# The store of the new x moved from SyncE to ScalarE in the finishes of the first three layers

## The chip, the cores and the metric

The kernel runs on one core of one Trainium2 chip. The metric is the device time of one execution in microseconds, the median of several runs. Engines: TensorE (PE in the profile, its weight loads PEld), VectorE (DVE), ScalarE (ACT), GpSimd (POOL) and SyncE (SP, which only issues transfers and waits). SyncE and ScalarE can both issue DMA transfers; each has a queue of its own. Sixteen DMA engines do the transfers.

## What is computed

x is 256 x 256 tokens of 64 channels in float32. Four layers run one after the other, each of the form x = x + layer(gn(x)), where gn normalizes groups of two channels over the whole picture. A layer, cut to what matters (layer 1; the others differ in masks, biases and in which token axis is summed over):

```python
xn = layer_norm(x, norm_a, norm_b)
left = (xn @ Wl + bl) * sigmoid(xn @ Wlg + blg)
right = (xn @ Wr + br) * sigmoid(xn @ Wrg + brg)
out_gate = sigmoid(xn @ Wog + bog)
out = einsum('bkjd,bkid->bijd', left, right) / n
out = layer_norm(out, on_a, on_b) * out_gate
return out @ Wo + bo          # x_new = x + this
```

The group norm of the next layer needs sums over all of the new x, so every layer ends with a full pass that also gathers these sums.

## The kernel before

x lives in DRAM (XT), paired so that 128 partitions hold 64 channels of two tokens. It is worked in 16 chunks (NCH) of 128 x 2048 float32, 1 MB each. A layer has these stages, each code of its own per engine: `prepare` (a few tiny operations that turn the sums in `stats` into the scale `cen`), `norm` (layer norm, stored to XH or XHA as two float16 parts), `project` and a contraction for the first 32 channels, the same for the other 32, and `finish`.

`finish` is the stage that the change touches. It is written out (no loop on the engines) for 64 tiles t of 128 x 512, four to a chunk c; every engine runs its own list of tiles with a lag, and semaphores join them. Per tile, in the first two layers (`gate_first`):

- TensorE: four transposes of the normalized sums (L1454), three float16 matmuls of the output gate (L1466), the output projection (L1473).
- ScalarE: the affine of the norm on the transposed sums (`scale_shift`, L1498; in the third and fourth layer a plain copy, L1502), the sigmoid of the gate (L1507), and seven tiles later the `square` of the new x with its sum (L1522), whose accumulator is read by an operation of its own.
- VectorE: the product with the gate (L1587), the add of the old x (L1594), which counts up `x_ready`, and once a chunk the subtraction of the mean (L1363, L1365). In the third layer VectorE applies the gate (L1602) and GpSimd adds the old x (L1556) and counts up `x_ready`.
- GpSimd, in the first two layers: the scaling of a chunk (L1547).

The new x of a chunk is made in place in the buffer into which the old one was loaded; four such buffers go round (`xi`, `x_of(c)`).

SyncE's list in a finish, per chunk c: load the kept sums of chunk c + 4 (L920; not in the first layer) after a wait for `consumed`; load the projected x of a chunk three later (L929, L932) after a wait for `gate_projected`; `store(c - 1)`, a wait for `x_ready` and the store of the new x (L1404); then, once the store of chunk c - 2 has landed and its squares are taken, load x of chunk c + 2 into the buffer that has come free (L936). After the last chunk SyncE waits for the first twelve stores, issues four loads for the next layer's first two chunks (L303, L299) and then the last store. The fourth layer stores its output instead (L1400).

At the end of a block all engines meet. In the next layer's `norm` SyncE, ScalarE and GpSimd wait at their start until all stores have landed (`stored`); GpSimd then sets four rows of constants (L709, L710), for which VectorE's first operation (L717) waits.

On entering the network (L485, L489) ScalarE copies x out of PSUM and stores eight chunks itself, in front of the first layer, while SyncE loads x.

Of the kernel before, what the change touches and what calls it, by code (L numbers as in the profile page):

```python
# [55 lines left out]
NCH = N * N // 2 // COLS  # L56
# [47 lines left out]
def build(nc, x_in, masks, consts, params, out):  # L104
    ctx = ExitStack()
    with ctx:
# [5 lines left out]
        def sem(name):  # L112
            s = Sem(ctx.enter_context(nc.semaphore(name)))
            sems.append(s)
            return s

        XT = nc.dram_tensor("XT", [NT, 8, P, COLS], F32).ap()
# [55 lines left out]
        def bank(i):  # L173
            return banks[i // 2][:, (i % 2) * BANK:(i % 2 + 1) * BANK]
# [6 lines left out]
        stored = [sem(f"stored{i}") for i in range(4)]  # L181
# [35 lines left out]
        tokens_ready = sem("tokens_ready")  # L217
        mean_off = sem("mean_off")
        gated_ready = sem("gated_ready")
        x_ready = sem("x_ready")  # L220
# [35 lines left out]
        def pair_chunk(dram, ut, vb):  # L256

            return dram[bass.ds(ut, 1), bass.ds(vb, 1), :, :].rearrange("t v p f -> p (t v f)")
# [23 lines left out]
        def pair_cols(buf, q):  # L282

            return buf.rearrange("p (g f) -> p g f", g=8)[:, :, 64 * q:64 * q + 64]
# [626 lines left out]
        def at(c):  # L911

            return c // 8, c % 8
# [4 lines left out]
        def load_os(sp, layer, homes, c):  # L918
            ut, vb = at(c)
            sp.dma_start(homes.os[c % 4].rearrange("p (s f) -> p s f", s=2),  # L920
                         OS[ut, vb::8, :, :, :].rearrange("s p q f -> p s (q f)")) \
                .then_inc(landed[c % 4].s, 16)

        def load_xh(sp, layer, homes, c):
            ut, vb = at(c)
            for part in range(2):
                buf = homes.xh[c % len(homes.xh)][part]
                if layer["k_is_b"]:
                    sp.dma_start(buf, XH[ut, :, part, :, vb, :, :].rearrange("c s g f -> c s (g f)")) \  # L929
                        .then_inc(loaded_xh[c % 4].s, 16)  # L930
                else:
                    sp.dma_start(buf, XHA[:, part, :, ut, 16 * vb:16 * vb + 16, :].rearrange("c s j a -> c s (j a)")) \  # L932
                        .then_inc(loaded_xh[c % 4].s, 16)

        def load_xt(sp, homes, c):
            sp.dma_start(homes.xt[c % len(homes.xt)], pair_chunk(XT, *at(c))).then_inc(loaded_xt[c % 4].s, 16)  # L936
# [430 lines left out]
        def finish(block, number, layer):  # L1367

            low, gate_first, end, homes = layer["low"], layer["gate_first"], number == len(LAYERS) - 1, Homes(number)  # L1370
            k_is_b = layer["k_is_b"]
            xi, xh, nrm, nat = homes.xt, homes.xh, homes.nrm, homes.nat
# [7 lines left out]
            out_nat = out.rearrange("o (t a) (s v) c -> t (o a) s (v c)", t=NT, s=2)  # L1380
# [6 lines left out]
            def x_of(c):  # L1387

                return homes.xo if end else xi[c % len(xi)]
# [4 lines left out]
            @block.sync  # L1394
            def _(sp):
                def store(c):
                    ut, vb = at(c)
                    if end:
                        sp.wait_ge(tokens_ready.s, tokens_ready.n + 4 * c + 4)
                        sp.dma_start(out_nat[ut, :, :, vb * 1024:(vb + 1) * 1024],  # L1400
                                     nat[c % 2].rearrange("p (s f) -> p s f", s=2)).then_inc(stored[c % 4].s, 16)
                    else:
                        sp.wait_ge(x_ready.s, x_ready.n + 4 * c + 4)
                        sp.dma_start(pair_chunk(XT, ut, vb), x_of(c)).then_inc(stored[c % 4].s, 16)  # L1404

                for c in range(NCH + 2):
                    if c + 4 < NCH and not low:

                        sp.wait_ge(consumed.s, consumed.n + 2 * c + 2)
                        load_os(sp, layer, homes, c + 4)  # L1410
                    if c < NCH and c + len(xh) < NCH:

                        sp.wait_ge(gate_projected.s, gate_projected.n + 4 * c + 4)
                        load_xh(sp, layer, homes, c + len(xh))
                    if end and 1 <= c <= NCH:
                        if c - 1 + len(xi) < NCH:

                            sp.wait_ge(x_ready.s, x_ready.n + 4 * c)
                            load_xt(sp, homes, c - 1 + len(xi))
                    if c >= NCH:  # L1420
                        continue
                    if c >= 1:
                        store(c - 1)
                    if not end and c >= 2 and c + 2 < NCH:

                        sp.wait_ge(stored[(c - 2) % 4].s, stored[(c - 2) % 4].n + 16 * ((c - 2) // 4) + 16)
                        sp.wait_ge(stats_taken.s, stats_taken.n + 4 * (c - 2) + 4)
                        load_xt(sp, homes, c + 2)
                if not end:
                    for h in range(4):  # L1430
                        sp.wait_ge(stored[h].s, stored[h].n + 48)
                    sp.wait_ge(turned.s, turned.n + tiles - 4)
                    for h in range(2):
                        load_xt_chunk(sp, h, h, LAYERS[number + 1]["k_is_b"])
                store(NCH - 1)
                if end:
                    for h in range(4):
                        sp.wait_ge(stored[h].s, stored[h].n + 4 * NCH)

# [53 lines left out]
            @block.scalar  # L1493
            def _(act):
                def scale_shift(t):
                    act.wait_ge(turned.s, turned.n + t + 1)
                    if gate_first:
                        act.activation(turn_bank(t), turn_bank(t), ACT.Identity, bias=vec(V_OB),  # L1498
                                       scale=vec(V_OW)).then_inc(scaled.s, 1)
                    else:  # L1500
                        act.wait_ge(out_projected.s, out_projected.n + t - 3)
                        act.activation(aff[t % 4], turn_bank(t), ACT.Copy).then_inc(scaled.s, 1)  # L1502

                def sigmoid(t):
                    act.wait_ge(gate_projected.s, gate_projected.n + t + 1)
                    act.wait_ge(gated_ready.s, gated_ready.n + t - 3)
                    act.activation(og[t % 4], bank(2 + t % 2), ACT.Sigmoid, scale=unscale).then_inc(gate_ready.s, 1)  # L1507

                def back(t):
                    c, q = divmod(t, 4)  # L1510
                    if q == 0 and c >= 2:
                        act.wait_ge(stored[(c - 2) % 4].s, stored[(c - 2) % 4].n + 16 * ((c - 2) // 4) + 16)
                    act.wait_ge(turned_back.s, turned_back.n + t + 1)
                    act.activation(nat[c % 2].rearrange("p (s v c) -> p v s c", s=2, c=C)[:, 4 * q:4 * q + 4, :, :],
                                   bank(t % 2).rearrange("p (j c s) -> p j s c", j=4, s=2),
                                   ACT.Copy).then_inc(tokens_ready.s, 1)

                def square(t):
                    c, q = divmod(t, 4)
                    act.wait_ge(x_ready.s, x_ready.n + t + 1)  # L1520
                    act.wait_ge(stats_taken.s, stats_taken.n + t)
                    act.activation(sum1[:, 0, N:2 * N].bitcast(BF16).rearrange("p (g f) -> p g f", f=64),  # L1522
                                   pair_cols(x_of(c), q), ACT.Square, bias=shift,
                                   accum_out=stats[:, t, 1:2]).then_inc(stats_taken.s, 1)

                def second_root(t):
                    if t == SECOND:
                        act.preload_act_table_set("natural_log_exp_and_others")
                        root(act, 1, MOMENTS - 2)
                        act.preload_act_table_set("sigmoid_and_others")  # L1530
                    if t == 2:
                        act.wait_ge(summed.s, summed.n)

                act.preload_act_table_set("sigmoid_and_others")
                if not end:
                    act.wait_ge(weights.s, weights.n)
                unrolled(tiles, (second_root, 0), (scale_shift, 0), (sigmoid, 0), *([] if end else [(square, SL)]),
                         *([(back, TBA)] if end else []))

# [184 lines left out]
```

## Time and profile before

| | us |
|---|---|
| median of 3 runs | 2210.91 |
| lowest, highest | 2204.99, 2215.15 |
| the profiled execution | 2208.5 |
| its span in the profile | 2206.5 |
| TensorE busy | 1972.7 |
| VectorE busy | 1735.3 |
| ScalarE busy | 1691.9 |
| GpSimd busy | 624.5 |

The three finishes that the change touches lie, in the profile, at about 442 to 583 us, 978 to 1113 us and 1520 to 1657 us; the fourth ends the kernel. The page has the engines' shares; the share of busy time of a stretch, in a view by windows, says which engine is full there; the timeline gives single operations with start and length; the view of waits names what ended an engine's idle time. An operation that starts before the one ahead of it on its engine has ended overlaps it.

### The profile page before, as it was taken

The numbers are of one execution on the slowest core, as the hardware profiler recorded it, in microseconds if no ns is written. First come the engines' busy times: TensorE is split into PE (matmuls) and PEld (weight loads), VectorE is DVE, ScalarE is ACT, GpSimd is POOL, SyncE is SP. The second block draws the span as 40 slices with busy tenths as digits, with TensorE's granted clock in tenths as the row PEclk, the third lists the DMA queues.
The fourth block names the chain that finished last, engine by engine and source line by source line (L and its number), as shares of the span: only waits on it lengthen the run. The fifth ranks groups of instructions, "written<-read, shape, count | busy, mean of one in ns | idle before, by whom it ended". The sixth has DMA issues, their size and how long they took to land. (4 is left out here: it accounts for less than half of the span.)

```text
span 2206.5 us, 46371 instructions
## 1 busy us (share of the span) xinstructions
PE 1972.7 (89%) x13956; PEld 1401.8 (64%) x13956; DVE 1735.3 (79%) x2934; ACT 1691.9 (77%) x2730; POOL 624.5 (28%) x590
## 2 busy tenths in 40 slices
PE   5798979699898998989989899899998989899998
PEld 4433959455433988965633598886553369798665
DVE  6788899989588977878958897877766888687665
ACT  3588869789888857759978785776997877596676
POOL 0100828265200000026410280742871000000655
PEclk8899999999999999999999999999999999999999
DMA  9488938279788928259969973917997984663798
GB/s 396 163 263 285 280 88 229 82 286 381 243 267 264 319 77 294 88 216 398 414 211 283 272 195 120 286 52 263 407 389 226 278 293 158 222 203 124 282 357 305
DMA packets 429367, 549.52 MB, mean 249 GB/s; under 512 B 14640, under 2 KB 325936, under 8 KB 412848
## 3 DMA queue, kind: packets, MB, share of 16 engines
q1 hardware_dynamic: 427648, 538.38, 72.6%
q10 hardware_dynamic: 1584, 9.51, 1.1%
q8 instruction: 64, 1.05, 0.2%
q14 instruction: 71, 0.58, 0.1%
HBM read 371.67 MB, written 176.16 MB: 248 GB/s over the span
## 5 line engine op out<-in xcount | busy, mean ns | idle before, releaser
L798 PE MATMUL bank<-whigh,kept 128*128 128x128 f16 x4096 | 507.7, 228 | 62.2 <-DMA kept<-XH 21.7
L798 PEld LDWEIGHTS bank<-whigh,kept 128*128 128x128 f16 x4096 | 466.5, 125 | 69.7 <-issue 56.2
L798 PE MATMUL bank<-wlow,kept 128*128 128x128 f16 x4096 | 506.7, 227 | 0.0
L798 PEld LDWEIGHTS bank<-wlow,kept 128*128 128x128 f16 x4096 | 467.1, 125 | 0.0
L1556 POOL TENSOR_TENSOR LR<-LR 128x512 f32<-128x512 f32 x128 | 186.6, 1477 | 526.9 <-DVE LR L1602 507.4
L820 ACT ACTIVATE sigs<-bank,small 128x256 f32<-128x256 f32 x512 | 236.7, 475 | 64.4 <-PE bank L798 58.0
L1547 POOL TENSOR_TENSOR LR<-LR,sum 128x2048 f32<-128x2048 f32 x30 | 136.6, 4553 | 510.7 <-DVE LR L1365 510.7
L662 PE MATMUL bank<-LR,cen 128*128 128x512 f32 x512 | 254.6, 623 | 20.9 <-DMA LR<-XT 8.6
L820 ACT ACTIVATE squares<-bank,small 128x256 f32<-128x256 f32 x512 | 236.1, 475 | 13.3 <-PE bank L798 5.6
L669 PE MATMUL bank<-LR,kst 128*128 128x512 f32 x512 | 240.9, 593 | 5.2 <-ACT LR L690 5.2
L835 POOL TENSOR_TENSOR msgs<-sigs,mask_sb 128x256 f32<-128x256 f32 x192 | 125.9, 670 | 381.8 <-ACT sigs L820 375.3
L864 DVE SCALAR_TENSOR_TENSOR LR<-bank,small,squares 128x256 f32 x512 | 222.8, 477 | 2.1 <-ACT squares L820 1.0
L1454 PEld LDWEIGHTS bank<-kst,LR 128*128 128x128 f32 x1024 | 151.7, 193 | 113.6 <-issue 90.6
L1466 PE MATMUL bank<-LR,wog 128*128 128x512 f16 x768 | 213.6, 388 | 5.5 <-ACT msgs L1507 5.5
L662 PEld LDWEIGHTS bank<-LR,cen 128*128 128x128 f32 x512 | 93.0, 196 | 170.1 <-issue 82.1
L690 ACT ACTIVATE LR<-bank,epsx 128x1024 f32<-128x1024 f32 x128 | 142.5, 1113 | 57.2 <-PE bank L669 57.2
L669 PEld LDWEIGHTS bank<-LR,kst 128*128 128x128 f32 x512 | 96.9, 190 | 129.0 <-issue 122.5
L1454 PE MATMUL bank<-kst,LR 128*128 128x128 f32 x1024 | 160.6, 281 | 17.5 <-ACT sigs L1502 11.2
L966 PE MATMUL bank<-LR 128*128 128x256 f32 x768 | 169.6, 383 | 5.2 <-DVE LR L864 5.2
L1221 PE MATMUL bank<-LR 128*128 128x256 f32 x768 | 166.6, 380 | 5.2 <-DVE LR L864 5.2
L684 ACT ACTIVATE LR<-bank,small 128x1024 f32<-128x1024 f32 x128 | 141.3, 1104 | 31.0 <-PE bank L662 30.1
L966 PEld LDWEIGHTS bank<-LR 128*128 128x128 f32 x768 | 146.6, 192 | 25.3 <-DVE LR L864 5.6
(174 smaller groups left out, 3745.3 us busy)
## 6 DMA issues: line engine op xcount, KB each, us to landing
kept<-XH SPq DMA_DIRECT2D x128, 512.0 KB, 5.5
LR<-XT SPq DMA_DIRECT2D x64, 1024.0 KB, 9.4
kept<-XHA SPq DMA_DIRECT2D x128, 512.0 KB, 4.6
LR<-XT SPq DMA_DIRECT2D x112, 512.0 KB, 5.5
XT<-LR SPq DMA_DIRECT2D x56, 1024.0 KB, 8.4
LR<-XH SPq DMA_DIRECT2D x64, 512.0 KB, 6.6
LR<-XHA SPq DMA_DIRECT2D x64, 512.0 KB, 5.8
OS<-kept SPq DMA_DIRECT2D x12, 2048.0 KB, 7.6
```

The source lines that it names most:

```text
L662: last = pe.matmul(to, cen[:, :], cols, start=True, stop=True)
L669: last = pe.matmul(banks[3][:, u * BANK:(u + 1) * BANK], K(K_MEAN), sq[t % 2][:, u * BANK:(u + 1) * BANK], start=True, stop=True)
L684: act.activation(sq[t % 2], banks[t % 3][:, :], ACT.Square, bias=cb).then_inc(squared.s, 1)
L690: act.activation(lnv[t % 2], banks[3][:, :], ACT.Ln, bias=epsx[:, :], scale=1.0 / X_SCALE ** 2).then_inc(logged.s, 1)
L798: last = pe.matmul(bank(g)[:, j * P:(j + 1) * P], tokens, w[:, half * P:(half + 1) * P], start=part == 0, stop=part == 1)
L820: act.activation(sig[g], bank(g).rearrange("p (m c) -> p c m", m=4)[:, C:, :], ACT.Sigmoid, scale=unscale).then_inc(gates_ready.s, 1)
L864: dve.scalar_tensor_tensor(dest[:, kt, :, bass.ds(m, 4)], bank(g).rearrange("p (m c) -> p c m", m=4)[:, 0:C, :], unscale, gate[g], ALU.mul ...
L966: last = pe.matmul(banks[e % 3][:, c * N:(c + 1) * N], src[:, kt, off_a + ch, ut * P:(ut + 1) * P], src[:, kt, off_b + ch, :], start=kt == ...
L1221: last = pe.matmul(banks[e % 3][:, c * N:(c + 1) * N], src[:, kt, off_a + 4 * g + c, ut * P:(ut + 1) * P], src[:, kt, off_b + 4 * g + c, : ...
L1454: last = pe.transpose(by_token(turn_bank(t))[:, :, j, :], n_t[c % len(nrm)][:, :, 4 * q + j], K(K_IDENT))
L1466: last = pe.matmul(bank(2 + t % 2), wog[w][:, :], pair_cols(x, q) if k_is_b else by_b(x, q), start=(w, part) == (0, 0), stop=w == 1)
L1556: pool.tensor_tensor(by_b(x_of(c), q) if end else by_token_cols(x_of(c), q), by_token(gated[t % 4]), by_token_cols(xi[c % len(xi)], q), AL ...
```

## The change

In the first three layers SyncE no longer stores the new x. ScalarE issues the store of a chunk directly behind the square of the chunk's fourth tile, with no wait of its own, and with the same semaphore (`stored`). SyncE's list has loads only; its waits for `stored` and `stats_taken` ahead of the loads of x stay. The fourth layer is as before.

```diff
@@ -1395,13 +1395,9 @@
             def _(sp):
                 def store(c):
                     ut, vb = at(c)
-                    if end:
-                        sp.wait_ge(tokens_ready.s, tokens_ready.n + 4 * c + 4)
-                        sp.dma_start(out_nat[ut, :, :, vb * 1024:(vb + 1) * 1024],
-                                     nat[c % 2].rearrange("p (s f) -> p s f", s=2)).then_inc(stored[c % 4].s, 16)
-                    else:
-                        sp.wait_ge(x_ready.s, x_ready.n + 4 * c + 4)
-                        sp.dma_start(pair_chunk(XT, ut, vb), x_of(c)).then_inc(stored[c % 4].s, 16)
+                    sp.wait_ge(tokens_ready.s, tokens_ready.n + 4 * c + 4)
+                    sp.dma_start(out_nat[ut, :, :, vb * 1024:(vb + 1) * 1024],
+                                 nat[c % 2].rearrange("p (s f) -> p s f", s=2)).then_inc(stored[c % 4].s, 16)
 
                 for c in range(NCH + 2):
                     if c + 4 < NCH and not low:
@@ -1419,7 +1415,7 @@
                             load_xt(sp, homes, c - 1 + len(xi))
                     if c >= NCH:
                         continue
-                    if c >= 1:
+                    if end and c >= 1:
                         store(c - 1)
                     if not end and c >= 2 and c + 2 < NCH:
 
@@ -1432,8 +1428,8 @@
                     sp.wait_ge(turned.s, turned.n + tiles - 4)
                     for h in range(2):
                         load_xt_chunk(sp, h, h, LAYERS[number + 1]["k_is_b"])
-                store(NCH - 1)
                 if end:
+                    store(NCH - 1)
                     for h in range(4):
                         sp.wait_ge(stored[h].s, stored[h].n + 4 * NCH)
 
@@ -1522,6 +1518,8 @@
                     act.activation(sum1[:, 0, N:2 * N].bitcast(BF16).rearrange("p (g f) -> p g f", f=64),
                                    pair_cols(x_of(c), q), ACT.Square, bias=shift,
                                    accum_out=stats[:, t, 1:2]).then_inc(stats_taken.s, 1)
+                    if q == 3:
+                        act.dma_start(pair_chunk(XT, *at(c)), x_of(c)).then_inc(stored[c % 4].s, 16)
 
                 def second_root(t):
                     if t == SECOND:
```

## Rows read from the trace of the kernel before

**Rows 1.** The page, part 1: busy time, share of the span, instructions of each engine.

```profile
PE 1972.7 (89%) x13956; PEld 1401.8 (64%) x13956; DVE 1735.3 (79%) x2934; ACT 1691.9 (77%) x2730; POOL 624.5 (28%) x590
```

**Rows 2.** Busy time by windows, in the first (two), second and third finish.

```profile
core 0: us, PE busy (x) PEld busy (x) DVE busy (x) ACT busy (x) POOL busy (x), PEclk, DMA share, GB/s
450.00:500.00 50.00, 46.58 (x205) 27.38 (x204) 44.38 (x83) 42.46 (x82) 33.79 (x13) 0.97 0.79 281
500.00:574.00 74.00, 72.51 (x334) 44.05 (x333) 66.16 (x127) 73.99 (x152) 36.45 (x8) 1.00 0.94 365
1034.00:1104.00 70.00, 69.74 (x323) 42.50 (x322) 63.01 (x122) 70.00 (x146) 34.57 (x8) 1.00 1.00 410
1587.00:1649.00 62.00, 60.12 (x272) 35.39 (x271) 45.81 (x74) 57.88 (x124) 43.84 (x31) 1.00 0.99 403
```

**Rows 3.** Timeline of ScalarE in the first finish: start us, us, operation [idle before].

```profile
564.69 1.05 ACT L1498 ACTIVATE bank<-bank,prm 128x512 f32<-128x512 f32 x1
...
565.92 1.04 ACT L1522 ACTIVATE sum<-LR,small 128x512 bf16<-128x512 f32 x1
566.53 0.52 ACT L1522 ACTIVATION_READ_ACCUMULATOR sum<-LR,small 128x1 f32 x1
566.62 1.06 ACT L1498 ACTIVATE bank<-bank,prm 128x512 f32<-128x512 f32 x1
```

**Rows 4.** Timeline of TensorE at the same tile.

```profile
564.75 0.61 PE L1454 MATMUL bank<-kst,LR 128*128 128x128 f32 x4
565.20 0.81 PE L1466 MATMUL bank<-LR,wog 128*128 128x512 f16 x3
565.85 1.02 PE L1473 MATMUL bank<-sigs,prm 128*128 128x512 f32 x2
...
566.71 0.61 PE L1454 MATMUL bank<-kst,LR 128*128 128x128 f32 x4
```

**Rows 5.** Timeline of ScalarE in the third finish, after a stall.

```profile
1589.32 0.70 ACT L1502 ACTIVATE squares<-bank 128x512 f32<-128x512 f32 x1
...
1591.07 0.72 ACT L1502 ACTIVATE squares<-bank 128x512 f32<-128x512 f32 x1
```

**Rows 6.** Timeline of ScalarE and its queue (ACTq) on entering the network.

```profile
49.27 2.06 ACT L485 ACTIVATE kept<-bank 128x512 f32<-128x512 f32 x4 [1.75 <-DMA XT<-kept]
51.36 0.34 ACTq L489 DMA_DIRECT2D XT<-kept  x1
51.75 1.57 ACT L485 ACTIVATE LR<-bank 128x512 f32<-128x512 f32 x3 [0.42 <-ACT kept L485]
```

**Rows 7.** Timeline of SyncE's issues late in the second finish: start us, us.

```profile
1080.52 1.20 SPq L932 DMA_DIRECT2D LR<-XHA  x2
1082.00 0.54 SPq L1404 DMA_DIRECT2D XT<-LR  x1
...
1089.80 0.34 SPq L1404 DMA_DIRECT2D XT<-LR  x1
1094.86 0.33 SPq L936 DMA_DIRECT2D LR<-XT  x1
```

**Rows 8.** Waits from 1490 to 1680 us: total us, times, longest us.

```profile
POOL LR L1556 <- DMA LR<-XT: 2.6, 3, 1.0
```

**Rows 9.** Timeline of all engines where the third layer hands over to the fourth.

```profile
1655.34 1.72 SPq L1404 DMA_DIRECT2D XT<-LR  x1
...
1657.08 0.19 ACT L1522 ACTIVATION_READ_ACCUMULATOR sum<-LR,small 128x1 f32 x1
...
1663.38 1.80 POOL L709 MEMSET LR<- 32x2048 f16 x1 [8.44 <-DMA XT<-LR]
...
1668.62 1.80 POOL L710 MEMSET sum<- 32x2048 f16 x1
...
1671.25 1.28 DVE L717 SCALAR_TENSOR_TENSOR LR<-bank,small,LR 126x1024 f32<-126x1024 f32 x1 [9.63 <-ACT LR L694]
```

**Rows 10.** DMA issues from 2190 us to the end: count, KB each, median us to landing.

```profile
out<-LR SPq DMA_DIRECT2D x2, 1024.0 KB, 4.3
```

## The prediction

> **What bounds the kernel now.** I read the page first for the shares of the engines: TensorE is busy 89% of the span, VectorE 79%, ScalarE 77% [rows 1]. An average over unlike stages says little, so I then took the busy time by stretch for the three finishes that the change touches. In the later part of the first finish ScalarE works 73.99 of 74 us, in that of the second 70.00 of 70 us, while the DMA engines' share is 0.94 and 1.00 at 365 and 410 GB/s. In the first 50 us of a finish ScalarE has idle time (42.46 of 50), and in the third finish too (57.88 of 62) [rows 2]. So in two of the three finishes, ScalarE, TensorE and the DMA engines are all close to their limits together. The reader should see in these rows that ScalarE is the engine that receives work, and that it has next to no room in 144 us of them.
>
> Next the rhythm of one tile (64 tiles a finish, 4 to a chunk). On ScalarE, in the first finish, an affine (L1498) starts at 564.69 and the next at 566.62: 1.93 us a tile, with no idle time given in any row; the read of the accumulator that ends the square starts at 566.53, and the next affine 0.09 us later [rows 3]. On TensorE the transposes (L1454) start at 564.75 and 566.71: 1.96 us a tile [rows 4]. Both engines run at the same pace; ScalarE could do a tile some 0.03 us faster, 0.1 us a chunk. In the second finish two stores of x, one chunk apart, are issued at 1082.00 and 1089.80: 7.80 us a chunk, 1.95 a tile [rows 7]. In the third finish, where the affine is a plain copy (L1502), ScalarE catches up after a stall at 1.75 us a tile (1589.32 to 1591.07) [rows 5], so there it has 0.2 us of room a tile, 0.8 us a chunk.
>
> Last the waits that end with a transfer. In the stretch that holds the third finish only GpSimd's add waits for a load of x: 3 times, 2.6 us together, 1.0 at most [rows 8]. I found no such row for the first two.
>
> **What is removed.** SyncE loses 48 issues, 16 a finish, and with them the wait for x_ready ahead of each. Past that wait move the loads of x, of the projected x and of the kept sums, and at the end of a finish the four loads of the next layer's x, which stood behind the second to last store and ahead of the last. What can they gain? The only waits for a load are those 2.6 us [rows 8]; nothing else can get shorter by an earlier load. Nor do fewer bytes move: in the second finish the load of x issued at 1094.86 had waited for the store issued at 1082.00 to land, 12.9 us [rows 7], against 4.3 us for the stores at the very end of the kernel, which meet nearly empty queues [rows 10]. The difference is the queue of a saturated DMA system, and it stays. Gain: 0 to 2.6 us; I take 0, since the engines are still full (share 0.99) in the stretch where the waits are [rows 2].
>
> **What is added.** ScalarE gets 48 issues. No semaphore wait comes with them: the square before has waited for x_ready. Queued behind each is the next tile's affine or copy, whose readers are VectorE's gate and through it TensorE's output projection. The price: on entering the network ScalarE already issues stores of the same size. A group of copies starts at 49.27 and takes 2.06 us, to 51.33; the issue starts at 51.36, takes 0.34, and the next copy starts at 51.75 [rows 6]. That is 0.42 us from work to work, and it holds a wait for the copies that the new place doesn't have. In the new place the read of the accumulator goes in, the issue follows (0.03 + 0.34 + 0.05 = 0.42 us to the next affine) where 0.09 us passes today: 0.33 us more a chunk. Bounds of one issue: 0 if it runs wholly beside the engine's work, 0.42 if nothing overlaps. I take 0.33, as the row on the same engine is the nearest there is.
>
> What of that lies on the path:
> - First and second finish, full stretch: ScalarE needs 4 x 1.93 + 0.33 = 8.05 us a chunk where a chunk takes 7.80, so 0.25 shows. 144 us of such stretches hold about 19 chunks (74/7.8 + 70/7.8 = 18.5): 19 x 0.25 = 4.8 us.
> - Their other 13 chunks, in which ScalarE stalls in part: I take half, 13 x 0.12 = 1.6 us; bounds 0 and 3.3.
> - Third finish: 4 x 1.75 + 0.33 = 7.33, under 7.80. The issue is hidden by ScalarE's 0.8 us of room, 0; if that cover fails it costs 16 x 0.25 = 4.
> - Tails. After the last tile ScalarE does nothing but squares, and the last issue stands between the last square and the end of the block, where all engines meet: 0.33 for the last issue and about 0.15 for the one before, 3 x 0.48 = 1.4 us.
>
> The sum is 4.8 + 1.6 + 0 + 1.4 = 7.8 us.
>
> **The hand-over to the next layer.** The last store now leaves later. In the third finish it is issued at 1655.34; after the change behind the square whose accumulator is read at 1657.08, so near 1657.2, 1.9 us later [rows 9]. GpSimd waits for it with four memsets, the first at 1663.38, the last at 1668.62 + 1.80 = 1670.42, and VectorE's first scale, which needs them, starts at 1671.25: 0.83 us of cover. But today that store stands behind loads in its queue (8.0 us from 1655.34 to 1663.38); with a queue of its own it needs between 4.3 [rows 10] and 8.0, so it lands between 1661.5 and 1665.2. Bounds of the effect: 0 and 1.0 us; I take 0, since the loads ahead of it will have been issued earlier.
>
> The profiled execution took 2208.5 us (span 2206.5), 2.4 under the median of 2210.91. 2208.5 + 7.8 = 2216.3, and put on the median: 2210.9 + 7.8 = 2218.7, so 2219 us, 0.36% more. A measurement of this kernel can tell about 0.5%, 11 us, from no change; mine is a forecast of no difference that can be told, leaning slow.
>
> **The rivals.**
> 1. *The issue costs nothing.* ScalarE's operations overlap [rows 3] (each starts before the one before has ended: 565.92 + 1.04 is later than 566.62), so an issue may slip in beside the square. Against it: TensorE's pace of 1.96 leaves only 0.03 a tile, and the engine stood still for the issue on entering [rows 6]. Time: 2210.9 + 0 to 2, about 2212.
> 2. *Slower: issues collide.* SyncE's own issues vary: a pair of loads takes 1.20 us, a store right behind them 0.54 instead of 0.34 [rows 7], and the last store 1.72 behind the next layer's loads [rows 9]. If the two engines share what makes the descriptors, ScalarE stands still for SyncE's issue too. At half a pair, 0.6 us, in every second issue, an issue costs 0.33 + 0.3 = 0.63 on average, 0.55 a chunk on the path of the 32 chunks of two finishes (17.6) plus tails 1.4 and the third finish (7.00 + 0.33 + 0.6 = 7.93 in 8 chunks, 8 x 0.13 = 1.0): 20 us, 2231. It decides once an issue shows 0.35 us in each of those 32 chunks. The 0.34 us of a ScalarE issue [rows 6] speak against it, in a stage where SyncE issues loads of x as well.
> 3. *Slower: loads come late.* With a queue of their own the stores no longer stand behind the loads but share the DMA engines with them at once. The load of x issued at 1094.86 is the last of its finish; a store of 1 MB running beside it at 410 GB/s costs it 2.5 us. In two finishes, 5 us on top of mine: 2224. The page "DMA: Bandwidth & Descriptors" of the Trainium skill, section "Queues, rings and completion order", states that a DMA engine takes turns between queues by packet; that is this case. Against it: a slower chunk gives the transfers more time.
> 4. *Faster: the loads were in the way after all.* The 2.6 us of waits [rows 8] go, the issue is hidden, and the hand-overs gain a little each: 2210.9 - 2.6 - 2 = 2206.
>
> **How the numbers follow.** My case 0.50 (of which 0.10 beyond +11 us), rival 1 0.16, rival 2 0.12, rival 3 0.10, rival 4 0.12 (of which 0.07 beyond -11 us, by something that no row shows). Slower: 0.10 + 0.12 + 0.10 = 0.32; faster 0.07; same the rest, 0.61. Range: 2206 (rival 4) to 2231 (rival 2); left out are the outer halves of these two, about 0.13.
>
> **What would show it.** Right: the timeline of ScalarE shows 48 issues of about 0.34 us at L1522's end, the next affine 0.4 us after the accumulator read, 8.05 us a chunk late in the first and second finish and 7.8 in the third; the share of DMA stays near 1. Rival 1: 7.80 us a chunk in all. Rival 2: issues on ScalarE of 0.6 us and more. Rival 3: GpSimd or VectorE waiting for LR<-XT in the last chunks. Rival 4: a finish shorter than today's. Most likely to be wrong is the share of the issue that shows on the path, for TensorE and ScalarE are within 0.03 us a tile.

## The result and the profile after

The changed kernel takes 2213.77 us (median of 22 runs) against 2209.48 us for the kernel before in 22 runs on the same chips: a ratio of 1.0021, 95% interval 1.0012 to 1.0029, so 4.6 us slower (2.7 to 6.4). One of the 22 runs of the changed kernel took 4045.6 us; the ratio leaves it out. With so many runs the difference is told from no change. The profiled execution took 2210.07 us, its span is 2207.7.

The page of the changed kernel: part 1 (to set beside [rows 1]), part 3 with the two queues, and part 6 with the stores.

```profile
PE 1969.6 (89%) x13950; PEld 1398.4 (63%) x13956; DVE 1730.5 (78%) x2934; ACT 1692.1 (77%) x2730; POOL 623.2 (28%) x590
...
q1 hardware_dynamic: 420736, 488.04, 67.2%
q10 hardware_dynamic: 8496, 59.84, 6.6%
...
XT<-LR ACTq DMA_DIRECT2D x48, 1024.0 KB, 7.9
```

The change does what it says: 48 stores on ScalarE's queue. ScalarE's busy time is as before. By windows, the same stretches as in [rows 2]:

```profile
450.00:500.00 50.00, 46.17 (x202) 27.38 (x201) 44.34 (x83) 42.28 (x82) 33.81 (x13) 0.97 0.76 281
500.00:574.00 74.00, 72.48 (x333) 43.84 (x332) 66.06 (x127) 73.99 (x152) 36.46 (x8) 1.00 0.97 363
1034.00:1104.00 70.00, 66.48 (x300) 39.05 (x299) 60.13 (x116) 67.39 (x138) 33.38 (x8) 1.00 1.02 401
1587.00:1649.00 62.00, 58.20 (x268) 35.14 (x267) 42.24 (x73) 56.40 (x122) 38.54 (x28) 1.00 1.02 409
```

In the full part of the first finish ScalarE's busy time is the same, 73.99 us. In the second, where ScalarE worked 70.00 of 70 us, it now works 67.39: it waits, where it had been the full engine. So the loss is not more work on ScalarE.

I measure a finish from the start of the square of its tile 3 to that of its tile 63. For the second finish, in the timeline of ScalarE, kernel before:

```profile
996.49 0.72 ACT L1522 ACTIVATE sum<-LR,small 128x512 bf16<-128x512 f32 x1
...
1112.42 0.72 ACT L1522 ACTIVATE sum<-LR,small 128x512 bf16<-128x512 f32 x1
```

and changed:

```profile
995.34 0.72 ACT L1518 ACTIVATE sum<-LR,small 128x512 bf16<-128x512 f32 x1
...
1114.45 0.72 ACT L1518 ACTIVATE sum<-LR,small 128x512 bf16<-128x512 f32 x1
```

115.93 us have become 119.11. The same reading gives 117.63 and 117.71 for the first finish, 116.72 and 117.92 for the third: +0.1, +3.2 and +1.2, together 4.5 us. A second profiled execution of each kernel (e9 and e10, below) gives 0.0, +4.2 and +1.2. That 4.5 is so near to the measured 4.6 us is in part chance: the spans of the two profiled executions differ by 1.2 us only (2206.5 and 2207.7), so the stages outside the three finishes differ by 3.3 us the other way, and those stages vary by 3.9 us between the two profiled executions of the kernel before. What is sure is the second finish. What it waits for stands in its waits (changed kernel, 984 to 1122 us; there was no such row in this execution of the kernel before):

```profile
DVE LR L1592 <- DMA LR<-XT: 6.6, 5, 1.9
```

and for the third, where [rows 8] had 2.6 us (1490 to 1680 us):

```profile
POOL LR L1554 <- DMA LR<-XT: 22.0, 7, 5.4
```

The loads of x come late, in the chunks 10 to 14 of the second finish. Most of GpSimd's 22.0 us in the third doesn't show in its length, which grew by 1.2. In the timeline of the second finish two of these waits, each at the first add of a chunk:

```profile
1077.11 0.75 DVE L1592 SCALAR_TENSOR_TENSOR LR<-bank,prm,LR 128x512 f32<-128x512 f32 x1 [1.93 <-DMA LR<-XT]
...
1094.62 0.75 DVE L1592 SCALAR_TENSOR_TENSOR LR<-bank,prm,LR 128x512 f32<-128x512 f32 x1 [1.84 <-DMA LR<-XT]
```

And the store of x leaves much later than it did. The fifth of the second finish, in the timeline of the queues, before:

```profile
1025.21 0.53 SPq L1404 DMA_DIRECT2D XT<-LR  x1
1025.84 0.38 SPq L936 DMA_DIRECT2D LR<-XT  x1
```

and changed:

```profile
1029.38 0.35 SPq L936 DMA_DIRECT2D LR<-XT  x1
...
1031.94 0.34 ACTq L1522 DMA_DIRECT2D XT<-LR  x1
```

6.7 us later for the store, and 3.5 us for the load of x of the same round. The first store of that finish leaves 3.5 us later (994.85, below, against 991.33). The changed kernel's finish itself began 1.15 us sooner in these two executions (995.34 against 996.49), so on the finish's own clock the two stores are 7.9 and 4.7 us late, and the load 4.7. The square stands seven tiles behind the affine in ScalarE's list, so it comes long after x is ready, and longer still where ScalarE stops for the second root.

What a late store does is written in SyncE's waits (984 to 1122 us), before and changed: how long SyncE stood ahead of the load of x (L936) until the store from that buffer had landed.

```profile
SPq L936 <- DMA XT<-LR: 17.3, 6, 4.6
```

```profile
SPq L936 <- DMA XT<-LR: 57.8, 12, 7.8
```

SyncE works through its list in order, so behind each of these waits stand not only the load of x but also the loads of the kept sums (L920) and of the projected x (L932). Early in the second finish, on its own clock, the load of the kept sums that left at 11.9 us leaves at 15.4, the next at 25.3 instead of 22.0, then 34.4 instead of 29.8. The changed kernel's transfers from 1004 to 1054 us, in 40 slices of 1.25 us (first row: the DMA engines' busy share in tenths), show what that does:

```profile
DMA  8999987899999999999999999999999999999999
GB/s 251 426 431 410 426 275 128 328 275 306 410 398 418 418 400 416 223 405 408 405 428 423 436 428 352 354 442 393 413 400 442 334 347 378 388 423 360 252 374 433
```

The hole at the sixth to tenth slice (1010.25 to 1016.5 us, down to 128 GB/s) comes behind a stretch from 1006.1 to 1010.4 us in which SyncE issued nothing and waited for the store issued at 1002.65. In the kernel before, no slice is below 364 GB/s.

### The profile page after: what moved, and what is told of

Same layout as the page of the kernel before. It is cut to its first block and busy times, and to the rows that moved or that the text cites. A ratio compares the mean times of both kernels' runs of the same rounds, so it can differ in the third digit from the quotient of the medians.

```text
span 2207.7 us, 46365 instructions
## 1 busy us (share of the span) xinstructions
PE 1969.6 (89%) x13950; PEld 1398.4 (63%) x13956; DVE 1730.5 (78%) x2934; ACT 1692.1 (77%) x2730; POOL 623.2 (28%) x590
```

## The experiments

Three theories. **A, late stores**: SyncE may load x into a buffer only when the store from it has landed; a store that leaves late makes the load leave late, fewer bytes move early in a finish, and those put off are missing at its end, where the DMA engines are full. **B, two queues**: stores in a queue of their own take turns with the loads and hold them up, whenever they leave. **C, early loads**: SyncE, no longer held by the wait for x_ready, issues the loads of sums and projected x earlier, and they stand ahead of those of x.

The table has, for each kernel, the second and the third finish as measured above, VectorE's waits for loads of x in the second (984 to 1122 us), SyncE's waits for stores of x to land in the same stretch, what the DMA engines moved from 1004 to 1054 us, and the ratio to the kernel before with its interval. Two numbers are two profiled executions of the same kernel.

| kernel | second finish, us | third, us | waits for x, us | SyncE's waits for stores, us | GB/s | ratio |
|---|---|---|---|---|---|---|
| before, and again (e9) | 115.93, 116.01 | 116.72, 114.74 | 0, 1.3 | 17.3, 18.2 | 415, 412 | 1.0004 (0.9993 to 1.0016), e9 |
| e1: ScalarE, five tiles behind | 116.40 | 117.06 | 4.8 | 21.2 | 415 | 0.9998 (0.9984 to 1.0012) |
| e5: ScalarE, six | 116.72 | 116.28 | 4.7 | 37.7 | 409 | 1.0006 (0.9994 to 1.0017) |
| the change, and again (e10): seven | 119.11, 120.21 | 117.92, 115.98 | 6.6, 6.2 | 57.8, 57.5 | 374, 372 | 1.0021 (1.0012 to 1.0029); 1.0014 (1.0002 to 1.0027), e10 |
| e6: ScalarE, nine | 121.73 | 120.84 | 11.9 | 79.8 | 358 | 1.0064 (1.0042 to 1.0085) |
| e2: SyncE, about as late as the change | 119.94 | 117.67 | 10.4 | 9.7, and 70.1 held ahead of the stores | 372 | 1.0042 (1.0027 to 1.0057) |
| e3: the change, other loads held | 119.62 | 118.91 | 8.5 | 64.4 | 360 | 1.0023 (1.0011 to 1.0036) |
| e8: the change, few loads of sums | 115.91 | 114.75 | 0 | 40.0 | 355 | 0.9980 (0.9969 to 0.9991) |

The stretch from 1004 to 1054 us is fixed, while the second finish begins between 991.87 us (e5) and 1000.06 us (e2). Over the same 50 us of each finish, from 7.5 us behind the square of tile 3, e5 has 403 GB/s and the others are within 4 of the table.

**e1_sooner: the same store, two tiles sooner.**

```diff
-                    if q == 3:
-                        act.dma_start(pair_chunk(XT, *at(c)), x_of(c)).then_inc(stored[c % 4].s, 16)
+                def store_sooner(t):
+                    c, q = divmod(t, 4)
+                    if q == 3:
+                        act.wait_ge(x_ready.s, x_ready.n + t + 1)
+                        act.dma_start(pair_chunk(XT, *at(c)), x_of(c)).then_inc(stored[c % 4].s, 16)
...
-                         *([] if end else [(square, SL)]),
+                         *([] if end else [(store_sooner, 5), (square, SL)]),
```

> The store stays on ScalarE but moves two tiles up in its list (five tiles behind the affine instead of seven, ahead of the square), with a wait for x_ready of its own; all three finishes. Theory A (the stores leave too late: 3.5 to 6.7 us later than before, so the loads of x that wait for them are late too, the DMA engines are fed less early in a finish, and the bytes put off make loads late at its end): the second finish, 119.1 us from its first to its last chunk's last square after the change and 115.9 before, comes back to about 116, the waits for LR<-XT in it go from 6.6 us to under 1, and the time is within 2 us of the kernel before (about 2209 to 2211). Theory B (a queue of its own lets the stores take turns with the loads and holds these up, whenever the stores leave): the second finish stays at 118 to 119 us and the time at about 2214. Theory C (SyncE, free of the stores, issues the other loads earlier, and they stand ahead of those of x): as B.

The second finish is back at 116.40 us and the time at that of the kernel before. There are still two queues, and SyncE's list is that of the change: B and C both fall with this run, A stands. One number missed: 4.8 us of waits are left, where under 1 was expected, in three pieces, and they show little in the length of the finish (0.5 us).

**e2_sp_late: one queue, late stores.**

```diff
                         sp.wait_ge(x_ready.s, x_ready.n + 4 * c + 4)
+                        if 4 * c + 11 <= tiles:
+                            sp.wait_ge(gate_ready.s, gate_ready.n + 4 * c + 11)
                         sp.dma_start(pair_chunk(XT, ut, vb), x_of(c)).then_inc(stored[c % 4].s, 16)
```

> The kernel before, with the store on SyncE as it was, but held until ScalarE's sigmoid seven tiles on is done (gate_ready), which is when the changed kernel's ScalarE issues it. One queue, late stores. Theory A: the second finish gets longer than 115.9 us, to 118 to 121, with waits for LR<-XT, and the time is 2213 or more. Theory B: no second queue, so the second finish stays at 116 and the time at 2209 to 2211. Theory C: SyncE is held longer, so 116 too.

119.94 us with a single queue: a second queue isn't needed for the loss. The run isn't lateness of the stores alone, though. The first nine stores of the second finish leave 0.7 to 1.2 us later than in the change, and SyncE, which stands 70.1 us for the sigmoids (L1405), issues its loads of x and of the sums late for that reason, not only because a store hasn't landed. The time is worse than the change's (2218.51 us): after two of the three finishes VectorE's first sum of the next layer starts 3.9 us after the last square instead of 1.1, since here SyncE is late as well with its last issues (in the first finish until 586.85 us, 3.4 us after the start of the last square), and all engines meet at the end of the block.

The windows from 1004 to 1054 us: before, e1, the change, e2, e6 in this order (the last number is GB/s, the one before it the DMA engines' share).

```profile
1004.00:1054.00 50.00, 46.32 (x211) 27.51 (x210) 43.99 (x82) 47.45 (x94) 32.19 (x11) 1.00 1.02 415
```

```profile
1004.00:1054.00 50.00, 46.32 (x210) 27.67 (x209) 43.99 (x84) 47.58 (x94) 29.26 (x9) 1.00 1.02 415
```

```profile
1004.00:1054.00 50.00, 46.28 (x211) 27.63 (x209) 43.94 (x84) 47.42 (x94) 31.25 (x11) 1.00 0.99 374
```

```profile
1004.00:1054.00 50.00, 46.31 (x212) 27.80 (x211) 43.96 (x80) 47.45 (x96) 32.08 (x14) 1.00 0.98 372
```

```profile
1004.00:1054.00 50.00, 45.58 (x207) 26.98 (x205) 42.05 (x76) 47.45 (x94) 32.13 (x11) 1.00 0.95 358
```

The compute engines do the same work in this stretch in the first four kernels, but for GpSimd, whose stretch cuts its chunks at other places: the loss isn't made here, it is prepared here. 415 less 374 GB/s over 50 us are 2.05 MB, and 2.05 MB take 4.9 us at 415 GB/s: the second finish then loses 3.2 to 4.2 us.

**e3_held: SyncE's old wait put back, stores as in the change.**

```diff
+                    if not end and c >= 1:
+                        sp.wait_ge(x_ready.s, x_ready.n + 4 * c)
```

> The changed kernel, with SyncE's wait for x_ready of chunk c - 1 put back where its store stood: stores from ScalarE as changed, all other loads no earlier than before. Theory C: the second finish comes back to 116 us and the time to 2210. Theories A and B: it stays at 119 us or grows a little, the time at 2214.

119.62 us, 2214.58 us: as theory A has it. It is a weak test of C. The wait that was put back is nearly always met (1.5 us of waits for VectorE ahead of the loads of x in the whole stretch, and 8.3 at its end), since SyncE stands at the store's landing anyway, 64.4 us, and its early loads leave at the same points of the finish as the change's. Against C speak e1, and the loads named above: in the change those of the kept sums leave later than in the kernel before, not earlier, from the third one of the finish on.

**e4_first: the change in the first finish alone.** The conditions are `number > 0` for SyncE's stores and `number == 0` for ScalarE's.

> The change in the first layer's finish alone; the second and third as before. All theories: the loss is in the second and third finish, where the kept sums are loaded too and the DMA engines are full; here the time is that of the kernel before within 1 us (2209 to 2211), the first finish 117.7 us from its first to its last chunk's last square, as in both kernels. If the ScalarE issue costs something by itself (0.33 us a chunk, as predicted), the first finish would be some 4 us longer.

The ratio is 0.9991 (0.9978 to 1.0003). The first finish took 115.93 us here, not 117.7. That isn't the change: one chunk early in it takes about 10.1 or 11.8 us in any of the kernels, and the finish was 116.04 us in the kernel before run again. With 16 issues on ScalarE the full part of the finish keeps its 7.75 us a chunk.

**e5_lag6 and e6_lag9: the store six and nine tiles behind the affine.** As e1, with `(store_at, 6)` ahead of the square, and with `(store_at, 9)` behind it.

> As e1_sooner, with the store six tiles behind the affine: between e1 (five) and the change (seven). Theory A (late stores): the second finish, first to last chunk's last square, between e1's 116.4 and the change's 119.1 us, about 117.5; time about 2211. If it isn't the lateness that counts but some accident of these lists, there is no order in the three.

> The store nine tiles behind the affine, two later than in the change (3.9 us later at 1.95 us a tile), with the wait for x_ready that is long met. Theory A: the suspected cause doubled: the second finish grows beyond 119.1 us, to about 122, the third beyond 118 to about 121, and the time to 2219 or more. Theory B (a second queue is the harm, whenever the stores leave): as the change, 119 us and 2214.

Five, six, seven and nine tiles give 116.4, 116.7, 119.1 (120.2) and 121.7 us: the order is that of the lateness. It isn't a straight line; six costs far less than the 117.5 that was expected, and the step comes between six and seven. In part that is the place in the list: the store of six stands ahead of a square and that of seven behind one, so that in the even part of the second finish the store of chunk 8 leaves 62.6, 64.6 and 67.8 us after the square of tile 3 with five, six and seven, 2.0 us and then 3.2. SyncE's waits for stores grow with each step (21.2, 37.7, 57.8, 79.8 us). Nine makes the third finish long too (120.84) and the time 2221.58 us, as theory A had it. It even makes VectorE wait 9.0 us for loads of x in the first finish, where no kept sums are loaded and where the change costs nothing.

**e7_four_issues: what an issue costs ScalarE.** e4_first with three small transfers ahead of each store.

```diff
+                    for k in range(3 if number == 0 and q == 3 else 0):
+                        act.dma_start(SPARE[3 * c + k, :, :], kst[:, 0:16]).then_inc(spare.s, 16)
                     if number == 0 and q == 3:
                         act.dma_start(pair_chunk(XT, *at(c)), x_of(c)).then_inc(stored[c % 4].s, 16)
```

> e4_first (the change in the first finish alone) with three more transfers of 8 KB issued by ScalarE ahead of each store there, to a DRAM tensor that nobody reads: four issues in a row, some 1.4 us of ScalarE's queue a chunk. The prediction held that an issue adds 0.33 us of standing engine. If an issue costs that wherever it stands, the first finish grows by 3 x 0.33 x 10 to 16 chunks, 10 to 16 us, over e4's 116 to 117.7. If ScalarE's list runs ahead of its work by about 1.2 us (in the change's trace an issue starts 0.49 us before the square ahead of it in the list has begun), one or two issues are hidden and the rest shows: four cost 0.2 to 0.6 us a chunk, 2 to 9 us in all.

The timeline of ScalarE and its queue for one chunk:

```profile
549.55 0.95 ACTq L1529 DMA_DIRECT2D SPARE<-kst  x2
549.95 0.71 ACT L1510 ACTIVATE squares<-bank,small 128x512 f32<-128x512 f32 x1
550.52 0.75 ACT L1525 ACTIVATE sum<-LR,small 128x512 bf16<-128x512 f32 x1
550.52 0.51 ACTq L1529 DMA_DIRECT2D SPARE<-kst  x1
551.06 0.61 ACTq L1531 DMA_DIRECT2D XT<-LR  x1
551.13 0.23 ACT L1525 ACTIVATION_READ_ACCUMULATOR sum<-LR,small 128x1 f32 x1
551.72 0.75 ACT L1501 ACTIVATE bank<-bank,prm 128x512 f32<-128x512 f32 x1 [0.35 <-issue]
```

The four issues fill the queue from 549.55 to 551.67, 2.1 us, and the engine stands for 0.35 us of it. The first finish grows to 123.49 us, by 5.8 to 7.6 over the two lengths seen in the others, 0.4 us a chunk. So ScalarE has cover for one issue and not for four. The median time is 2218.22 us, about 11 over e4's, more than the finish explains; the profiled execution, 2211.51 us, is the fastest of the ten, and the rest I haven't traced.

**e8_no_os: the change without most loads of the kept sums** (for c of 4 and more, SyncE counts up the semaphore instead).

> The changed kernel without the loads of the kept sums beyond the first four chunks, in the second to fourth layer: 12 x 0.5 MB less in a finish, and old sums are used in their place, so part of the computation is left out. If the lost time is that of transfers in finishes whose DMA engines are full, nothing waits for LR<-XT in the second and third finish, the second finish is 115.9 to 116 us although the stores leave as late as in the change, and the time is 2205 to 2209. If ScalarE or the barrier costs it, the second finish stays at 119.

The stores leave as late as in the change, the DMA engines move only 355 GB/s, and yet the second finish is 115.91 us with no wait for x. SyncE waits 40.0 us for stores to land, more than in e5, and it costs nothing: lateness costs only where the bytes put off have no room later in the finish.

**e9, e10, e11: before, the change and e4 again.**

> The kernel before, once more, for the spread of the profiled finishes. The theory of the late stores needs the second finish to be a property of the kernel and not of the execution: 115.9 to 116.2 us here again, and no wait for LR<-XT in it; third finish 114.7 to 116.8; ratio 1.000 within 0.15%.

> The changed kernel once more: second finish 118.5 to 119.7 us, third 117 to 119, ratio 1.002. If the second finish comes out at 116 in this execution, the difference between the two profiles was chance and the theory of the late stores has lost its main row.

> e4_first once more, to tell whether its 0.9991 is a gain. Theory: nothing is gained, since no wait for a load ended in the first finish before; ratio 0.999 to 1.001, with an interval that holds 1. A gain of 0.1% would come from the next layer's x, loaded 8 us earlier.

The second finish belongs to the kernel: 116.0 before, 119.1 and 120.2 changed, and 115.9 to 116.1 in e4, e7 and e11, whose second finish is that of before. Missed were the 1.3 us of waits in e9, and the third finish of e10, 115.98 where 117 to 119 was expected: it spreads by 2 us from one execution to the next (before: 116.72 and 114.74), so I put no weight on single values of it. e11 has 0.9997 (0.9985 to 1.0009): the change in the first finish alone is no gain that can be told. None of the versions beats the kernel before beyond its interval, except e8, which leaves loads out.

## Why the prediction was right and wrong

**Right**: the side it leaned to, and the range. 4.6 us were measured where 7.8 were forecast. **Wrong**: that it could not be told from no change; and the mechanism. Every term of the 7.8 us (4.8 + 1.6 + 0 + 1.4) is the price of an issue on ScalarE, and each measured 0. The loss comes from a term that stood at nothing, the loads of x that leave late because the stores do. That the two numbers lie so near each other is luck.

**The price of an issue (0.33 us a chunk, 6.4 us in the two finishes) is 0.** The changed kernel's ScalarE at the first chunk of the second finish:

```profile
994.77 0.68 ACT L1503 ACTIVATE squares<-bank,small 128x512 f32<-128x512 f32 x1
994.85 0.34 ACTq L1522 DMA_DIRECT2D XT<-LR  x1
995.34 0.72 ACT L1518 ACTIVATE sum<-LR,small 128x512 bf16<-128x512 f32 x1
995.95 0.20 ACT L1518 ACTIVATION_READ_ACCUMULATOR sum<-LR,small 128x1 f32 x1
996.05 0.75 ACT L1494 ACTIVATE bank<-bank,prm 128x512 f32<-128x512 f32 x1
```

The issue starts 0.49 us before the square that stands ahead of it in the list, and has ended (995.19) before the square starts. The next affine starts 0.10 us after the read of the accumulator, against 0.09 in [rows 3], and a chunk of the full stretch takes 7.75 to 7.76 us from square to square in both kernels (the 7.80 was read from two stores), where 8.05 was forecast. I took the price from [rows 6], where the issue had a semaphore wait for the copies ahead of it; with that wait the issue can't start before the copies end, and stands between them and the next copy. Without it the issue runs beside the engine's work. I had named it ("a wait for the copies that the new place doesn't have") and yet kept the number. The lower bound, 0, was the value: rival 1 on this term. With it fall the halves for the other chunks, and the tails (1.4 us): VectorE's first sum of the next layer starts 1.1 us after the start of the last square in both kernels, in all three finishes. The rows also show that the order of ScalarE's list doesn't hold the store back until the square has run; by then the tile's x had been ready for over 4 us (SyncE stored it 5.2 us ahead of this square in the kernel before). Whether anything would hold the store back if x were not ready, no run shows. The Trainium skill, page "Perfetto Trace Analysis", section "Sequencer Loop", says that the sequencer pushes an engine's instruction into a queue and goes on to the next; the rows agree, and e7 shows how far that carries here.

**The hand-over (0 to 1.0, taken as 0) held.** From the next layer's first sum on VectorE to its first scale (L717) it is 14.8, 14.3 and 13.7 us before, 14.4, 14.5 and 14.6 changed, 14.2, 14.4 and 13.8 in e9, and 14.0, 13.8 and 14.0 in e10: no difference beyond the spread.

**The later store was priced in one place only.** The step on the hand-over worked out that the last store leaves 1.9 us later, and asked what that costs there. The same step for the other stores is missing: for 36 of them, the first twelve of each finish, a load of x waits until they have landed, and in the second finish they leave 4.4 to 7.9 us later on the finish's own clock. "What is removed" looked only at what the loads could gain, and took 0. SyncE's wait for a landed store stood in the trace of the kernel before, 17.3 us in the second finish; it became 57.8. The 3.2 to 4.2 us of the second finish are this term, and so, as far as one can tell with its spread of 2 us, are the 1.2 of the third.

**The rivals.** Rival 3 named the right place and sign (GpSimd or VectorE waiting for LR<-XT in the last chunks, 5 us in two finishes) by the wrong mechanism: e1 has two queues and 415 GB/s, and e2 has one queue and the loss. The page "DMA: Bandwidth & Descriptors" of the Trainium skill, section "Issuing engines are not separate DMA queues", holds that transfers of different engines share the same DMA engines and that issuing from several saves only issue time; e1's 415 GB/s agree. Rival 2 is out: the issues of the change took 0.34 to 0.36 us (up to 0.41 in e10). Of its idea there is something in e7, where issues right behind each other took 0.5 to 0.6.

**What stays open**: why packets take longer in the early stretch. The share of the DMA engines is 0.99 there at 374 GB/s and 1.02 at 415, with 4280 packets against 4752, and in the slice with 128 GB/s it is still 0.7 or more; that the bytes depend on when the stores leave is shown, how the engines come to be busy with fewer bytes is not. Why six tiles cost so little and seven so much isn't settled by the 3.2 us between their stores. And the stages outside the finishes, 3.3 us shorter in the changed kernel's profiled execution, haven't been traced.

## What to carry to other kernels

When a store moves to an engine that computes, ask first when it will leave and not what its issue costs: place it by the time at which the data is ready, five tiles behind and not seven here, and follow every load that waits for its buffer, and everything that stands behind that load in the list of the engine that issues it. A stage whose transfers just keep up has no slack for lateness at its start, though no compute engine shows it there: their waits appear some 50 us later, at the last loads. Look at the waits of the issuing engine instead. And the price of an operation read at another place of the trace holds only with the waits that stood around it there.

## What the runs showed of the hardware that I had not expected

- ScalarE issues a transfer up to 1.0 us before the operation ahead of it in its list has begun (0.49 us in the rows above; 1031.94 against 1032.94 for the fifth store of the same finish). One issue of 0.34 us a chunk costs nothing on an engine that is busy for 73.99 of 74 us; four in a row, 2.1 us, make it stand for 0.35 us.
- The DMA engines' share of busy time says little of what they move: 0.99 with 374 GB/s, 1.02 with 415, in the same stretch of the same work, and between 0.7 and 0.8 in a slice of 1.25 us with 128 GB/s.
- The same kernel's finishes differ from one execution to the next: the first by 1.7 us (115.9 or 117.7, one chunk of 10.1 or 11.8 us), the third by 2.0, while the second repeats within 0.15 us where its stores leave as before (115.9 to 116.1 us in five executions).
